# A tile of zeros multiplied in TensorE's waits, in a fused cross-attention and mixture-of-experts kernel

## The reference

```python
# x, ctx: (4, 512, 256); 16 heads of 16; windows of 64; 16 experts, 256 -> 1024 -> 256
q = layernorm(x) @ W_q.T + b_q;  k = ctx @ W_k.T + b_k;  v = ctx @ W_v.T + b_v
# each window of 64 queries sees its own and the previous window's keys, causal and masked
att = softmax(where(mask, q k^T / 4, min)) v          # per head
x = x + tanh(g_xattn) * (att @ W_o.T + b_o)
t = layernorm(x).reshape(2048, 256)
logits = t @ gate_w.T                                 # top 1 of 16 experts
# each expert takes its first 160 tokens, in order of tokens
out = weight * (gelu(t @ w1[e]) @ w2[e])              # for tokens with a place
x = x + tanh(g_ffn) * out
```

## Time and profile before

| | |
|---|---|
| median of 3 runs | 375.38 us (374.42 to 375.98) |
| the profiled execution | 374.38 us |
| its span, first to last instruction | 372.5 us |
| mean granted TensorE clock | 0.928 |
| busy: PE, DVE, ACT, POOL | 311.7, 186.4, 173.1, 147.1 us |

### The profile page before, as it was taken

How to read it: one execution, slowest core, us unless ns; L and a number is a source line. 1 busy time by engine, 2 the same in 40 slices (tenths; PEclk the granted TensorE clock), 3 DMA queues, 4 the chain that set the end, 5 groups by cost and what they waited for, 6 DMA issues and landing times.

```text
span 372.5 us, 8304 instructions
## 1 busy us (share of the span) xinstructions
PE 311.7 (84%) x2822; PEld 273.8 (73%) x2822; DVE 186.4 (50%) x908; ACT 173.1 (46%) x649; POOL 147.1 (39%) x177
## 2 busy tenths in 40 slices
PE   4839989999999999773650699999999999999980
PEld 3517757877587758662440699999999999999980
DVE  3787788999999899993230022221222122222210
ACT  2469999999999999881020011111111111111110
POOL 5539566578677467655004001111111111111111
PEclk9987999999999999997555599999999999999996
DMA  7801593159412021202013557888898888888300
GB/s 211 298 1 24 171 376 109 24 177 370 163 25 87 0 114 25 87 2 113 5 52 113 138 171 232 277 274 271 270 284 264 267 271 275 264 275 270 124 14 11
DMA packets 39252, 60.52 MB, mean 162 GB/s; under 512 B 3192, under 2 KB 27674, under 8 KB 39216
## 3 DMA queue, kind: packets, MB, share of 16 engines
q1 hardware_dynamic: 35856, 53.28, 45.6%
q0 software_dynamic: 2816, 6.25, 4.9%
q10 hardware_dynamic: 544, 0.52, 0.4%
HBM read 44.60 MB, written 14.19 MB: 158 GB/s over the span
## 4 chain that ended last, share of the span: by engine, by line
PE 53%; DVE 16%; ACT 11%; issue 9%; POOL 5%; DMA 3%; SPq 0%; POOLq 0%; DVEq 0%
PE bank L1325 20%; PE bank L1338 18%; ACT probs L552 8%; DVE probs L718 4%; POOL expert_queue L443 3%; DVE rows L785 2%; PE bank L1052 2%; DVE probsT L737 2%; PE bank L1138 2%; PE bank L1348 2%; DMA ctx_rows<-in_ctx_dram 2%; PE bank L1030 1%; PE bank L1102 1%; PE bank L1308 1%; PE bank L1071 1%
## 5 line engine op out<-in xcount | busy, mean ns | idle before, releaser
L552 ACT ACTIVATE probs<-probs,low 128x128 f32<-128x128 f32 x256 | 99.2, 401 | 5.2 <-DVE low L718 5.2
L648 ACT ACTIVATE w_raw<-bank 128x480 f32<-128x480 f32 (+1 forms) x48 | 25.3, 526 | 137.5 <-PE bank L1325 137.5
L488 POOL DMA_INDIRECT out_dram<-q_rows,place x32 | 29.2, 912 | 135.8 <-issue 109.6
L1325 PE MATMUL bank<-xdT,w 128*128 128x160 f32 x512 | 80.0, 306 | 0.7 <-DVE xdT L955 0.7
L430 POOL TENSOR_TENSOR probs<-probs,r_total 128x512 f32<-128x512 f32 x64 | 66.1, 1050 | 35.5 <-DVE r_total L727 35.4
L1325 PEld LDWEIGHTS bank<-xdT,w 128*128 128x128 f32 x512 | 73.5, 195 | 0.9 <-issue 0.9
L1338 PE MATMUL bank<-w_raw,w 128*128 128x160 f32 x512 | 72.2, 299 | 0.0
L1338 PEld LDWEIGHTS bank<-w_raw,w 128*128 128x128 f32 x512 | 70.4, 190 | 0.0
L718 DVE CUSTOM_DVE_ANT_0 probs<-bank,mask_now 128x128 f32<-128x128 f32 x256 | 57.5, 283 | 6.5 <-PE bank L1071 6.1
L552 ACT ACTIVATION_READ_ACCUMULATOR probs<-probs,low 128x1 f32 x256 | 51.5, 201 | 0.0
L961 DVE COPY yT<-bank 128x320 f32<-128x320 f32 x16 | 7.9, 492 | 77.4 <-PE bank L1338 77.4
(11 more groups left out here) (110 smaller groups left out, 384.9 us busy)
## 6 DMA issues: line engine op xcount, KB each, us to landing
w<-in_L_ffn_w_dram SPq DMA_DIRECT2D x32, 1024.0 KB, 5.7
expert_queue<-empty_row SPq DMA_DIRECT2D x1, 5140.0 KB, 17.9
q_rows<-expert_queue SPq DMA_DIRECT2D x16, 321.2 KB, 5.8
ctx_rows<-in_ctx_dram SPq DMA_DIRECT2D x4, 512.0 KB, 9.8
out_dram<-rows SPq DMA_DIRECT2D x4, 512.0 KB, 4.2
x_all<-in_x_dram SPq DMA_DIRECT2D x3, 512.0 KB, 7.1
v_shift<-v SPq DMA_DIRECT2D x12, 128.0 KB, 2.2
x_all<-in_x_dram SPq DMA_DIRECT2D x2, 256.0 KB, 3.7
```

Source lines behind the costliest of these rows:

```text
L488: pool.indirect_dma_start(out=out_rows, out_offset=bass.IndirectOffsetOnAxis(ap=place[i][:, s:s + 1], axis=0), in_=q_rows[i][:, s, D:2 * D ...
L552: last = act.activation(probs[:, i % NP_, j], probs[:, i % NP_, j], ACT.Exp, scale=-1.0, bias=low[:, i % NP_, j:j + 1], accum_out=total[:, ...
L648: act.activation(hidden[:, ms[0]:ms[-1] + 1, :], ps_hidden[m][:, 0:n].rearrange("p (m c) -> p m c", c=CAP), ACT.Gelu_apprx_tanh).then_inc( ...
L1325: last = pe.matmul(ps_hidden[m][:, c * CAP:(c + 1) * CAP], w1_sb[i % 2][:, k, f * P:(f + 1) * P], xdT[i % 2][:, k], start=(k == 0), stop=( ...
```

## The change

A tile of zeros, `idle_rows`, is set by POOL ahead of its other constants. TensorE multiplies it at 18 places, each time with all of its 512 columns and with its first 128 as weights, into a PSUM bank that nobody holds at that point; nothing reads the result. Each call of `keep_warm(ps, times)` issues `times` such bf16 matmuls, unconditionally, in TensorE's order. In the last wait, up to the first gathered rows, the calls follow POOL's issues of the last batch's scatters by a new semaphore. One old wait, for the last batch's scores to be taken, is moved from in front of `project` to in front of `probsT_of` 14.

```diff
+        idle_rows = sb("idle_rows", [P, 512], BF16)
...
+            pool.memset(idle_rows[:], 0.0).then_inc(idle_ready, 1)
             pool.memset(ident[:], 0.0)
...
+                    if n == LAST:
+                        pool.sem_inc(scatter_begun, 1)
...
+            def keep_warm(ps, times):
+                for _ in range(times):
+                    pe.matmul(ps[:], idle_rows[:, 0:P], idle_rows[:], start=True, stop=True)
...
+            pe.wait_ge(idle_ready, 1)
+            keep_warm(bank[3], 7)
             pe.wait_ge(consts_ready, 1)
             wT_of(0, bank[4])
+            keep_warm(bank[3], 2)
             wT_of(1, bank[5])
+            keep_warm(bank[3], 3)
             for k in range(KD):
                 ctxT_of(0, k, bank[k])
+            keep_warm(bank[3], 3)
             for k in range(KD):
                 xnT_of(0, k, bank[6 + k])
+            keep_warm(bank[3], 2)
             k_of(0, 0, bank[3])
             q_of(0, 0, bank[2])
...
             attend(LAST, 2)
+            pe.wait_ge(scores_taken, B * UNITS)
+            keep_warm(ps_scores[3], 3)
             probsT_of(LAST, 14)
+            keep_warm(ps_scores[3], 4)
             probsT_of(LAST, 15)
+            keep_warm(ps_scores[3], 2)
             pe.wait_ge(x1_ready, value(LAST, 2, 1))
             x1nT_of(LAST, 0)
+            keep_warm(ps_scores[3], 3)
             pe.wait_ge(att_taken, value(LAST, CHUNKS, 3))
             attend(LAST, 3)
-            pe.wait_ge(scores_taken, B * UNITS)
+            keep_warm(ps_scores[3], 4)
             project(LAST, 1)
+            keep_warm(ps_scores[3], 13)
             x1nT_of(LAST, 1)
+            keep_warm(ps_scores[3], 2)
             route(LAST)
+            keep_warm(ps_scores[3], 4)
             count(LAST)
+            keep_warm(ps_misc, 10)
+            for t in range(T):
+                pe.wait_ge(scatter_begun, t + 1)
+                keep_warm(ps_misc, 5 if t < T - 1 else 22)
```

More of the change, by code:

```diff
@@ L179, in flamingo_kernel @@
         y_out = [sem(f"y_out{i}") for i in range(NQ)]
+        idle_ready, scatter_begun = sem("idle_ready"), sem("scatter_begun")
         const_step, consts_ready, empty_ready = sem("const_step"), sem("consts_ready"), sem("empty_ready")
```

## The result

The changed kernel takes 369.21 us (median of 7 runs, 366.61 to 370.43) against 375.23 (7 runs): ratio 0.984, 95% interval 0.982 to 0.986, or 6.0 us less. The forecast was 7.4 less and 368.0. The profiled execution of after took 366.61 (span 364.9, mean granted clock 0.973 for 0.928), the fastest of the seven, so its profile shows more of the gain than a usual run has. That difference became the main question.

The account below looks back on a forecast made before the run. Low-clock TensorE work on the chain before PE-bound experts was taken as the bound. 4.71 + 0.33 + 2.46 - 0.1 = 7.4 us off the profiled 374.38 gave 367.0, or 368.0 as median; range 366.4 to 371.8.

Parts of the forecast that it names:

- What bounds it: Slow-clocked TensorE is on the chain before the experts; the experts are PE-bound, so gains before them reach the end whole.
- Rival E: The earlier experts wait for weights, which takes the whole gain: 375 us; chance 0.04.
- A filler's cost: Each multiplication of zeros takes 0.213 us at the full clock, 0.43 at the low one.
- Rival D: A filler costs more: at 0.32 us 2.8 lost, 370.8; at 0.43 us 377.7; chance 0.06, mostly near 0.32.
- Fillers fit their waits: Tail and last-wait fillers stay hidden, except two ahead of route (+0.43 us); the last wait has 0.8 us to spare.
- Gains on the chain: The full clock saves 4.7 us up to route, 0.33 at xdT and 2.46 on the first 24 products.
- The front: 17 early fillers could start first queries 0.7 us earlier, but the DVE's normalisation of batch 1 covers it: 0 gained.
- The clock stays up: Fillers hold the granted clock at 1.00 from 168 us to the experts; the forecast's chance was 0.57.
- B: The clock still falls in probsT 15's wait, only 0.85 of 3.54 us filled: 5.0 us gained, 370.4; chance 0.22.
- The time: The whole kernel gains 7.4 us: 367.0 us in the profiled execution's terms, 368.0 as the median.

Follow-up runs that it names:

- fuller: Changed kernel with the last batch's waits filled further (15 fillers for 4 ahead of probsT 15) and none ahead of route: 373.1 us, ratio 0.985 to before.
- after_again: The changed kernel, unchanged, timed again on another call: 372.7 us against before's 378.3, ratio 0.985.
- after_third: The changed kernel, unchanged, timed a third time: 368.5 us against before's 375.3, ratio 0.981.
- trimmed: Changed kernel without front and route fillers, zeros set behind POOL's constants, other filler counts adjusted (10 for 4 ahead of probsT 15): 367.3 us, ratio 0.978 to before.
- front_only: Changed kernel with only the 17 front fillers and the memset, none from the last batch on: 374.9 us against before's 375.4, ratio 1.000.
- fuller_gap: fuller with 26 more fillers behind the first queries of group 1: 373.7 us against before's 378.3, ratio 0.988.
- transposes: Changed kernel with each multiplication of zeros replaced by two fp32 transposes of zeros, the first seven by five: 373.0 us, ratio 0.986 to before.
- trimmed_again: The same kernel as trimmed, timed once more: 371.4 us against before's 378.5, ratio 0.981.
- tail_only: Changed kernel without the 17 front fillers, the memset kept: 371.3 us against before's 375.4, ratio 0.989.

## Why the prediction was right, and where it was off

- **What bounds it.** Right. All of the gain is between 168 us and the first products, and the experts kept it: 162.7 or 162.8 us in nine of the fourteen profiles, and the other five are those with slow first products. Rival E is out.
- **A filler's cost.** Right: 0.213 forecast. In fuller 19 last 4.26 and 15 last 3.40, so 0.215 each. The Trainium skill's 215.7 ns (TensorE: Matmul & The Clock Gate, Part 1) agrees with that. Rival D is out.
- **Fillers fit their waits.** Right that they fit, but the last wait was mis-sized. The prediction let the last 22 begin at the end of the last scatter and had 0.8 us to spare. The increments come earlier than the scatters they follow: in after's chain the first two stand at 191.49 and 192.74, ahead of the scatters recorded at 191.73 and 193.10. So the fillers ran on almost without a hold, and ended 2.3 to 2.7 us before the rows where all of them were quick (after_again, after_third, trimmed). after had only 1.5, since its first fillers there were slow. This is the rest in which after_third's clock fell. POOL's increments cost nothing, not 0.1: its scatters start 1.28 us apart, as in before.
- **Gains on the chain**, forecast against after's profile: first x1n transposes 0.46 and 0.46; attend 3 0.89 and 0.86; projection 1.86 and 1.76 (3.77 to 2.01); second transposes 0.46 and 0.46; route net 1.04 and 1.10 (3.24 to 1.71 + 0.43); xdT 0.33 and 0.30; products 2.46 and 2.22 (5.72 to 3.50). Together 7.2 against 7.4. These are the gains of an execution that kept its clock from 168 to 187. The products' term was sized by a row from the steady stage, 1.63 for 12; the first group includes its start and takes 3.50.
- **The front.** Right, 0, and for the reason given: in front_only TensorE's first queries start at 12.59 for 13.24, 0.65 us earlier for a forecast of 0.7, and the DVE's first look does not follow them.
- **The clock stays up.** This is the step that failed, in part. The first profile bears it out between 168 and 187, by luck in probsT 15's wait, as shown above; the usual execution does not. Eight later profiles have the fillers upstream (fuller and fuller_gap aside), and in all eight the first x1n transposes or attend 3 are slow. Six of them leave 2.7 us of probsT 15's wait empty, as the prediction did: in five the clock fell in that rest or within a microsecond behind it, as B had it, in the sixth (transposes) 2.3 us behind its end. The two with 1.4 us empty (trimmed and trimmed_again) fell 2.3 and 2.1 us behind its end too. The three with 1.0 us or less (after, fuller, fuller_gap) did not fall there. B was given 0.22 and its fall was the commoner case. But its price was wrong too, 2.4 us; after_again's fall of that kind cost 1.2, since the clock was back before the projection and not in its middle. The other costs that I had not listed are a fall at route (tail_only, with the former 1.4) and one behind the last filler (after_third, 3.0).
- **The time.** 6.0 won for 7.4. The tails of after, after_again, after_third, tail_only and transposes average 31.2 against before's 35.1, 3.9 won. The experts give 2.5 where the clock held and 1.9 on average over the same five profiles, so 5.8 to 6.4, about the median's 6.0. 7.4 is about what an execution without a costly fall wins (the profiled one, 7.8).

## What to carry to other kernels

Filling TensorE's waits with spare multiplications pays where slow matmuls are on the chain of waits and nowhere else: look for that before filling (here the front's were not). Fill a wait nearly to its end, but count the fillers so that a late TensorE still fits, since each one beyond the wait costs its full 0.215 us. Compare how much of each wait is left empty with what was planned, before a kept clock is taken as shown. Judge such a change by many executions, because where the clock falls differs between them: the first profiled execution of the changed kernel was 2.6 us below its median, the third 3.1 above.

## What the runs showed of the hardware

- The clock fell in stretches in which TensorE was partly at work. In after it fell at 163.9, where PE had been busy in half of the time and had never idled longer than 1.1 us, ahead of every filler of the tail. Stretches of after:

```profile
160.00:164.00 4.00, 2.06 (x45) 1.59 (x38) 3.89 (x20) 4.00 (x21) 1.52 (x2) 0.99 0.01 4
164.00:168.00 4.00, 4.00 (x16) 3.28 (x15) 2.19 (x9) 1.39 (x7) 2.63 (x3) 0.58 0.00 0
```

The projection in it took 3.47 us for 1.89, and cost nothing, since POOL was last at probsT 15. In before's profile the same place kept its clock, with PE busy just as long (2.07 us of the 4 from 160). So these figures do not tell the two apart. Its waits were not filled: the score banks are still being read there, and no fit place was tried.

- The reading of 1.00 in the first microseconds is not a measurement. In after, four transposes took 1.09 us at 4.47, with the reading at 1.00, and eight took 1.04 at 7.63.
- On two of the chips before itself took 378.3 and 378.5 us, otherwise 375.2 to 375.4. In the profiles from those two chips the first stage is longer, from the DVE's first look to POOL's last normalisation 153.9 to 155.9 us, for 150.8 to 151.7 in the others; tail and experts are not. All five of them, and none of the other nine, have two long waits of the DVE ahead of the attention's copy (L755), for which the view names no engine of this core. Timeline, DVE, after_again and then after:

```profile
101.84 0.48 DVE L755 TENSOR_SCALAR attT<-bank,parity_mask 128x256 f32<-128x256 f32 x1 [2.52 <-remote]
...
99.30 0.48 DVE L755 TENSOR_SCALAR attT<-bank,parity_mask 128x256 f32<-128x256 f32 x1 [0.31 <-PE bank L1112]
```

The products with the values that it needs were done by 99.6 in after_again as well. The second such wait, near 141 us, is 2.3 us. What holds the DVE there was not tried.
